# Paired groups: chunk 2's x turned to tokens by VectorE, and the low part of the gated y made by GpSimd

## The reference

```
x  = hidden_states;  xn = layernorm(x)
# mixer
gate, hbc, dt = split(xn @ in_proj_w.T)
xBC = silu(causal_conv4(hbc));  xs, B, C = split(xBC)
dt = softplus(dt + dt_bias);  dA = exp(-exp(A_log) * dt)
state = state * dA + (dt * xs) outer B;   y = state . C          # over the tokens
y = y + D * xs
yn = y * rsqrt(mean over a group of y*y + eps) * norm_weight * silu(gate)
mixer = yn @ out_proj_w.T
# feed-forward: xn @ W_base.T + b_base + top-2 routed LoRA (8 experts, rank 16)
out = x + mixer + ffn
```

## Time and profile before

| what | value |
|---|---|
| median of three runs | 3192.64 us |
| span of the profiled execution | 3192.9 us |
| TensorE busy | 3175.7 us, 99% |
| VectorE busy | 2256.7 us, 71% |
| ScalarE busy | 1548.4 us, 48% |
| GpSimd busy | 829.9 us, 26% |
| chain of waits that ended last | TensorE 97%, VectorE 2% |
| granted TensorE clock, mean | 0.999 |
| mean length of a VectorE 32-row transpose | 303 ns, 672 of them |

### The profile page before, as it was taken

The page is one execution under the profiler, slowest core; times in us unless marked ns, Lnnn a source line. Parts: engine busy times, 40 slices in busy tenths (PEclk is TensorE's granted clock), DMA queues, the critical chain, the costliest instruction groups (busy, mean ns, idle before and its releaser), DMA issues.

```text
span 3192.9 us, 55463 instructions
## 1 busy us (share of the span) xinstructions
PE 3175.7 (99%) x18080; PEld 2616.4 (82%) x18080; DVE 2256.7 (71%) x4101; ACT 1548.4 (48%) x3816; POOL 829.9 (26%) x917
## 2 busy tenths in 40 slices
PE   8999999999999999999999999999999999999999
PEld 7878888887888888888888888888878888888887
DVE  7977777786587677777548767777755877776773
ACT  5666666663355444444235545444423545444441
POOL 4444434343032222222103222222210212122220
PEclk9999999999999999999999999999999999999999
DMA  7777777776655555556465555555556655555554
GB/s 288 279 256 263 267 274 266 269 267 245 239 207 185 186 185 191 185 187 206 157 236 200 188 182 186 191 184 192 192 171 233 204 182 186 189 190 193 182 187 159
DMA packets 185669, 672.66 MB, mean 211 GB/s; under 512 B 21056, under 2 KB 22208, under 8 KB 185408
## 3 DMA queue, kind: packets, MB, share of 16 engines
q1 hardware_dynamic: 161280, 584.91, 52.7%
q10 hardware_dynamic: 24128, 84.42, 7.6%
HBM read 532.41 MB, written 136.84 MB: 210 GB/s over the span
## 4 chain that ended last, share of the span: by engine, by line
PE 97%; DVE 2%; issue 0%; DMA 0%; ACT 0%; POOL 0%; ACTq 0%; SPq 0%; DVEq 0%; POOLq 0%
PE dense L1038 27%; PE dense L1040 27%; PE dense L1039 27%; PE pY L1136 3%; PE pD L1166 2%; PE pD L1136 1%; PE pX L1108 1%; PE dense L1075 1%; PE pU L1038 1%; PE pS L1040 1%; PE pCB L1113 1%; PE pS L1038 1%; PE pS L1039 1%; PE pU L1040 1%; PE pU L1039 1%; DVE conv_us L1448 1%
## 5 line engine op out<-in xcount | busy, mean ns | idle before, releaser
L1038 PE MATMUL dense<-xn_hi,w_hl 128*128 128x512 f32 (+1 forms) x2888 | 1143.9, 396 | 1.2 <-ACT conv_us L702 0.8
L1040 PE MATMUL dense<-xn_hi,w_hl 128*128 128x512 f32 (+1 forms) x2888 | 1125.2, 390 | 0.0
L1039 PE MATMUL dense<-xn_lo,w_hl 128*128 128x512 f32 (+1 forms) x2888 | 1123.4, 389 | 0.0
L1040 PEld LDWEIGHTS dense<-xn_hi,w_hl 128*128 128x128 f32 (+1 forms) x2888 | 540.1, 187 | 116.3
L1038 PEld LDWEIGHTS dense<-xn_hi,w_hl 128*128 128x128 f32 (+1 forms) x2888 | 540.7, 187 | 114.4 <-issue 2.9
L1039 PEld LDWEIGHTS dense<-xn_lo,w_hl 128*128 128x128 f32 (+1 forms) x2888 | 540.9, 187 | 110.9 <-issue 1.9
L1448 DVE SCALAR_TENSOR_TENSOR conv_us<-conv_in,const_g,conv_us 128x512 f32<-128x512 f32 x576 | 466.5, 810 | 164.0 <-ACT conv_us L683 150.3
L1038 PE MATMUL dense<-z_hi,w_hl 128*128 128x512 f32 x1024 | 406.7, 397 | 2.5 <-DVE acc L1588 2.0
L1588 DVE TENSOR_TENSOR acc<-acc,dense 128x512 f32<-128x512 f32 x256 | 175.7, 687 | 322.3 <-PE dense L1040 312.0
L1040 PE MATMUL dense<-z_hi,w_hl 128*128 128x512 f32 x1024 | 400.0, 391 | 0.0
L1039 PE MATMUL dense<-z_lo,w_hl 128*128 128x512 f32 x1024 | 399.6, 390 | 0.0
(11 more groups left out here) (202 smaller groups left out, 4427.6 us busy)
## 6 DMA issues: line engine op xcount, KB each, us to landing
w_hl<-w_split SPq DMA_DIRECT2D x732, 512.0 KB, 3.5
w_split<-w_hl SPq DMA_DIRECT2D x244, 512.0 KB, 3.6
cum_b<-cum_scratch ACTq DMA_DIRECT2D x128, 512.0 KB, 4.9
w_raw<-w_slots_dram SPq DMA_DIRECT2D x122, 512.0 KB, 5.2
acc<-x_tr_dram ACTq DMA_DIRECT2D x16, 512.0 KB, 6.9
out_tr_dram<-acc ACTq DMA_DIRECT2D x16, 512.0 KB, 4.7
BC<-x_tok_dram SPq DMA_DIRECT2D x6, 512.0 KB, 4.6
conv_us<-x_tok_dram SPq DMA_DIRECT2D x6, 512.0 KB, 5.7
```

Source lines behind the costliest of these rows:

```text
L1038: nc.tensor.matmul(out, lhs[0], rhs[0], start=start, stop=False)
L1039: nc.tensor.matmul(out, lhs[0], rhs[1], start=False, stop=False)
L1040: return nc.tensor.matmul(out, lhs[1], rhs[0], start=False, stop=stop)
```

## The change

In paired groups VectorE transposes x of chunks 0, 2 and 3, so TensorE transposes only that of chunk 1, and dtx, wx and xD of chunk 2 are made from x_tm. The calls of `x_rows` for chunk 2 stood in VectorE's program already and did nothing. The low part of the gated y is made by GpSimd (`z_low`), in places of its own order; the calls of `gated_lo` leave VectorE's paired groups.

```diff
-        BY_DVE = (0, 3)
+        BY_DVE = (0, 2, 3)
...
+                def z_low(g, c):
+                    pool.wait_ge(zhi_done, chunk(q, g, c) + 1)
+                    cs = slice(c * Q, (c + 1) * Q)
+                    nc.gpsimd.tensor_tensor(z_lo[:, :, cs], z_t[:], z_hi[:, :, cs].bitcast(F32), ALU.subtract)\
+                        .then_inc(z_done, 1)
...
                 def paired_group(g, p, last=False):
                     chunk_pre(g, p, 0)
                     wx_low(g, 0)
+                    z_low(g - 1, 3)
                     chunk_pre(g, p, 1)
                     wx_low(g, 1)
                     inv_rms(g, 0, True)
                     inv_rms(g, 1, True)
                     chunk_pre(g, p, 2)
                     wx_low(g, 2)
+                    z_low(g, 0)
                     chunk_pre(g, p, 3)
+                    z_low(g, 1)
                     wx_low(g, 3)
...
                     inv_rms(g, 2, True)
                     inv_rms(g, 3, True)
-                    if last and not last_block:
-                        ln_inv(q + 1, 2)
-                        ln_inv(q + 1, 3)
+                    z_low(g, 2)
+                    if last:
+                        if not last_block:
+                            ln_inv(q + 1, 2)
+                        z_low(7, 3)
+                        if not last_block:
+                            ln_inv(q + 1, 3)
...
-                    gated_lo(g - 1, 3)
...
-                    gated_lo(g, 0)
...
-                    gated_lo(g, 1)
...
-                    gated_lo(g, 2)
...
-                        gated_lo(7, 3)
```

## The result

The changed kernel takes 3212.20 us (median of 4 runs, 3210.87 to 3212.91), the kernel before 3193.14 us beside it (4 runs). The ratio is 1.0058, 95% interval 1.0047 to 1.0070: slower by 19.1 us, where +13.6 was forecast. The profiled execution took 3212.91 us, with a span of 3211.1 us.

The account below looks back on a forecast made before the run. TensorE's own queue was taken to bound the kernel; 20 groups at +0.70 us less 0.43 for the last gave +13.6, so 3192.6 became 3206 us; range 3182 to 3214, 3202 to 3210 for the forecast alone.

Parts of the forecast that it names:

- What bounds it, and what leaves TensorE: TensorE's own queue sets the time; four transposes leave it per paired group, 0.43 us each group, 9.0 us in all.
- Three portions at nothing: Three of VectorE's four portions (four 32-row transposes, 1.25 us each) stand next to output additions and cost nothing.
- The portion in front of dtx: Chunk 2's fourth portion, behind the second y addition, moves dtx 1.28 us later, from 65.96 to 67.24.
- The two races: Chunk 2: GpSimd's power starts 0.03 us ahead of VectorE's dtx, then S_lo 0.03 to 0.04 ahead of xD; GpSimd wins both.
- The durations behind the races: Chunk 2: S_dec ends at 68.82, xD starts at 69.69 and takes 1.80 us, the seventh output addition ends at 72.10.
- The restart: TensorE goes on 0.04 us after the seventh output addition, at 72.14, plus about 0.1 for a slower first spacing.
- The sum: All paired groups: +0.70 us in each of 20, -0.43 in the last, +13.6 us in all; chance 0.50.
- The 21st group: The last group of block 3 has its power 0.07 us later, behind dtx, and so gains 0.43 us.
- clock loss: Rival: the clock falls after each TensorE pause, 1.7 us more per stalled group, 34 in all, 3240 us; chance 0.04.
- The mixed case: Rival: the race falls differently in a third of the groups; +6.8 us, 3199, band 3187 to 3202; chance 0.10.
- GpSimd's new work at no cost: The 87 z_lo subtractions of 1.30 us each fit into GpSimd's idle time and cost nothing.
- z_lo in front of wx_lo of chunk 3: Rival: this z_lo on GpSimd becomes the wait, up to 21 x 1.0 us on top, 3204 to 3227; chance 0.04.

Follow-up runs that it names:

- e3: The changed kernel with VectorE's addition of the seventh output tile put ahead of xD in chunk 2; 3186.02 us, ratio 0.9982.
- e8: e3 with z_lo back on VectorE; 3183.57 us, ratio 0.9971.
- e6: The changed kernel with chunk 2's fourth portion of transposes made beside its third, ahead of the y work, not in front of dtx; 3182.73 us, ratio 0.9970.
- e5: The changed kernel with all transposes on VectorE kept, but chunk 2's dtx, wx and xD read pX, which TensorE makes again; 3193.20 us, ratio 1.0002.
- e12: e6 with chunk 1's x also turned by VectorE and, in that chunk, the third output tile's first addition ahead of xD; 3187.46 us, ratio 0.9982.
- e2: The kernel before with only z_lo moved from VectorE to GpSimd; 3192.54 us, ratio 1.0000.
- e4: The changed kernel with xD of chunk 2 right behind wx, ahead of the two operations on pCB; 3195.70 us, ratio 1.0010.
- e9: The changed kernel with GpSimd's S_lo in front of C_lo in chunk 2; 3202.29 us, ratio 1.0031.

## Why the prediction was right

- **What bounds it, and what leaves TensorE.** Right. 84 instructions fewer, and where nothing waits the transposes are worth 0.44 us per group: in e3 and e8 TensorE's first x unit starts at +5.74 in place of +6.18, and in e6 the period falls from 89.59 to 89.15 in block 3. 21 of these are 9.2 us, and e6 gained 9.5.
- **Three portions at nothing.** Right: e5 carries all four and takes 3193.2.
- **The portion in front of dtx.** The mechanism was right and the size off: +1.28 was taken, and dtx moved from +0.61 to 66.98 - 64.96 = +2.02 us behind the y addition, 1.41 later. The portion starts 0.72 behind the y addition (64.96 to 65.68), 0.03 after its end, where the forecast had 0.60, as an ordinary operation follows and as the portion behind the seventh addition does in the earlier trace rows (69.10 to 69.71). Both occur in the changed kernel: 84 portions start 0.71 to 0.72 behind the operation before them and 42, all behind an output addition, 0.60 to 0.61. What decides it was not found. These 0.13 us run unchanged through wx, xD, the addition and the restart.
- **The two races.** Both fell as forecast, in all 21 groups. The first was right in part by luck: the 0.13 us that the forecast had left out made the power's lead 66.98 - 66.83 = 0.15 us and not 0.03. A lead of 0.03 would not have settled it: S_lo wins with one in the earlier trace rows, but in one group of e12 GpSimd's wx_lo, ahead by as much, was the one held up (in GpSimd's and then VectorE's timeline):

```profile
3081.87 1.86 POOL L502 TENSOR_TENSOR wx_lo<-wx,wx_hi 128x512 fp32r<-128x512 f32 x1 [2.19 <-ACT wx_hi L751]
...
3081.90 0.68 DVE L1520 TENSOR_TENSOR w_raw<-x_tm,D_g 128x512 f32<-128x512 f32 x1
```

  The second is the precedent of the earlier trace rows to the hundredth: S_lo 0.04 ahead, xD 1.80.
- **The durations behind the races.** S_dec was to end 3.47 us behind the y addition and ends at 1068.57 - 1064.96 = 3.61; xD was to start at +4.34 and starts at +4.48; TensorE was to restart at 72.14 - 65.35 = +6.79 and restarts at +6.93. Each is the same 0.14 late.
- **The restart.** The addition ends at 71.83 and TensorE starts at 71.89, 0.06 later (0.04 was taken); its first spacing is 0.34 instead of 0.23 us, for which I had 0.1, and the next ones, 0.23 to 0.24, are also a little long.
- **The sum.** Per group 0.74 for the unit's start, 0.11 for the spacing and some hundredths behind it, as the group period shows: 90.49 against 89.59 us in block 3, +0.90. The forecast had +0.70; the terms that were too small are the start of the portion (0.13 of the 0.20) and, for the rest, the restart and the slower spacings behind it. The 21st group was to gain and stalled too: there the power is 0.07 later, but so is dtx. 20 x 0.70 - 0.43 = 13.6 becomes 21 x 0.90 = 18.9, of 19.1 measured. The time lay in the wide range (3182 to 3214) and above the forecast's own (3202 to 3210).
- **The rivals.** No clock loss: from 1072.00 to 1075.40, right behind the pause, the clock is at full speed, 2.4 GHz:

```profile
1072.00:1075.40 3.40, 3.40 (x15) 2.81 (x16) 3.30 (x9) 0.41 (x1) 0.54 (x1) 1.00 0.86 260
```

(columns: the stretch, its length, the busy time of PE, PEld, DVE, ACT and POOL, the granted clock, the DMA share and GB/s). The mixed case did not occur. GpSimd's new work at no cost was right (e2, 3192.54 us). z_lo in front of wx_lo of chunk 3 is in time, in GpSimd's and then TensorE's timeline:

```profile
1093.77 1.30 POOL L507 TENSOR_TENSOR z_lo<-z_t,z_hi 128x512 fp32r<-128x512 f32 x1
1095.57 1.29 POOL L502 TENSOR_TENSOR wx_lo<-wx,wx_hi 128x512 fp32r<-128x512 f32 x1 [0.51 <-ACT wx_hi L751]
...
1097.39 0.40 PE L1052 MATMUL pU<-wx_lo,B_hi 128*128 128x512 f32 x1
```

wx_lo waits for ScalarE's wx_hi and not for z_lo, and ends at 1096.86, 0.53 before its use.

On the rule of the Trainium skill (SBUF — State Buffer, "Who interferes with whom") that the first to issue holds the shared ports for its whole instruction: e6 agrees. wx begins at 65.05 and keeps its 0.69 us, and the power, begun at 65.25, takes 0.88 in place of 0.55. The changed kernel agrees as well, with S_lo ahead of xD by 0.04. The two rows of e12 above, with GpSimd ahead by 0.03 and VectorE served first, do not agree if the recorded start is taken for the issue; as with the earlier trace rows, starts this close in the trace do not tell who issued first.

## What to carry to other kernels

Moving an operand from PSUM to SBUF, or the work from TensorE to VectorE, can cost nothing in VectorE's own queue and still put its readers in the way of GpSimd: look in the timeline for what GpSimd does in the 2 us around each new reader, and which of the two is queued behind the other. Then order the queue by who is waited for: an operation that frees a PSUM bank for the engine that sets the time belongs ahead of one that may be held up (e3, +19 us turned into -6.6), or the held one belongs where it comes first (e6, -9.5). Slack that the trace shows in one group is not there in every group, and neither is the order in which the two engines meet: look at every group before moving more work (e12).

## What the runs showed of the hardware

- In the sequences of the changed kernel, e4 and e9, where each engine has an operation ready when the other finishes, the two take turns: S_dec, wx, C_lo; then S_lo, xD. In the changed kernel xD, begun at 69.44 beside S_lo (69.40 to 70.69), ends 0.55 us after it, as dtx did in the earlier trace rows.
- A VectorE operation with one input in PSUM is not held: 0.67 us inside S_lo in e3; in e5 dtx, wx and xD take 0.68 to 0.69 with S_dec, C_lo and S_lo beside them.
- 21 pauses of TensorE of 1.0 us (1.4 us between starts) never lowered the granted clock. Longer ones did not either: at the place of the earlier trace rows all twelve other traces have a pause of 1.30 to 1.78 us with the clock at 1.00, 2.4 GHz, behind it (e9, after 1.78 us, below), and so have the two pauses of 1.4 us in e3. Only the one of 2.0 us in before stood ahead of 3.4 us at 0.50, 1.2 GHz. No run here lies between 1.78 and 2.0.

```profile
167.60:171.00 3.40, 3.40 (x15) 2.83 (x16) 0.61 (x2) 3.40 (x7) 1.77 (x2) 1.00 0.81 265
```

- VectorE's first transposes of a group start 1.7 to 4.1 us late in 6 of the 21 groups (the third and the fifth of each block), the same six in every kernel, before included, with "issue" as the note. Nothing in the records names the cause, and no run here took it apart.
